# Graph attention on one core: the adjacency rounds taken from behind head 0, two splits moved later, two masks given to VectorE, and filler matmuls in head 0

## The reference

```python
seq = (x @ W_seq).reshape(N, H, DH)
score1 = jnp.einsum('nhd,d->hn', seq, a1)
score2 = jnp.einsum('nhd,d->hn', seq, a2)
scores = leaky_relu(score1[:, :, None] + score2[:, None, :], 0.2)
scores = scores + (1.0 - adj)[None, :, :] * -65500.0
attn = softmax(scores, axis=-1)
hidden = einsum('hij,jhd->ihd', attn, seq).reshape(N, D)
out = layernorm(x + elu(hidden @ W_out + b_out))
```

## Time and profile before

| | |
|---|---|
| median of 3 runs | 538.84 us (537.93 to 538.99) |
| the profiled execution | 538.96 us |
| its span, first to last instruction | 537.0 us |
| mean granted TensorE clock | 0.979 |
| TensorE busy | 513.0 us, 96% |
| VectorE busy | 472.1 us, 88% |
| ScalarE busy | 449.9 us, 84% |
| share of TensorE in the chain that ended last | 72% |

### The profile page before, as it was taken

The page is one execution under the profiler, slowest core; times in us unless marked ns, Lnnn a source line. Parts: engine busy times, 40 slices in busy tenths (PEclk is TensorE's granted clock), DMA queues, the critical chain, the costliest instruction groups (busy, mean ns, idle before and its releaser), DMA issues.

```text
span 537.0 us, 15347 instructions
## 1 busy us (share of the span) xinstructions
PE 513.0 (96%) x6778; PEld 463.7 (86%) x6778; DVE 472.1 (88%) x701; ACT 449.9 (84%) x487; POOL 32.1 (6%) x64
## 2 busy tenths in 40 slices
PE   9999997779999999999999999999999999999993
PEld 7888876669999999999999999999999999744542
DVE  3265999868999989999999999999999899888886
ACT  2677897799998899999999999999997869356664
POOL 3000000000000000000000000000000000024542
PEclk9999999589999999999999999999999999999997
DMA  8999972220202202021020201102022040014443
GB/s 287 374 395 324 362 184 39 84 80 2 80 2 81 81 2 80 2 81 49 35 80 2 81 9 73 81 2 81 2 81 79 4 139 2 1 59 141 134 138 117
DMA packets 30434, 52.76 MB, mean 98 GB/s; under 512 B 18336, under 2 KB 19616, under 8 KB 26400
## 3 DMA queue, kind: packets, MB, share of 16 engines
q1 hardware_dynamic: 29816, 51.26, 28.1%
q10 hardware_dynamic: 552, 0.52, 0.3%
HBM read 43.25 MB, written 4.33 MB: 89 GB/s over the span
## 4 chain that ended last, share of the span: by engine, by line
PE 72%; ACT 17%; DVE 9%; issue 2%; POOLq 0%; POOL 0%; ACTq 0%; DVEq 0%
PE sums L438 31%; PE bank L454 17%; ACT tring L569 12%; PE sums L509 10%; PE sums L361 9%; DVE tring L747 2%; ACT low L624 1%; PE sums L346 1%; ACT Vp L603 1%; DVE Vp L823 1%; PE bank L497 1%; PE sums L338 1%; DVE tring L742 1%; ACT tring L536 1%; DVE xp L817 1%
## 5 line engine op out<-in xcount | busy, mean ns | idle before, releaser
L569 ACT ACTIVATE tring<-abc,ab 128x2048 int8<-128x2048 f32 x149 | 290.3, 2028 | 0.0
L438 PE MATMUL sums<-Vp,tring 128*128 128x132 f16 x4096 | 249.0, 223 | 13.0 <-DVE tring L747 9.3
L438 PEld LDWEIGHTS sums<-Vp,tring 128*128 128x128 fp8e4 x4096 | 241.5, 99 | 17.8 <-DVE tring L747 12.6
L747 DVE TENSOR_TENSOR tring<-adj,tring 128x512 uint32<-128x512 uint32 (+1 forms) x265 | 168.2, 666 | 16.5 <-ACT tring L569 16.3
L454 PE MATMUL bank<-Vp,adj 128*128 128x132 f16 x2048 | 126.7, 222 | 0.7 <-DVE Vp L823 0.7
L454 PEld LDWEIGHTS bank<-Vp,adj 128*128 128x128 fp8e4 x2048 | 122.9, 97 | 1.2 <-DVE Vp L823 1.1
L742 DVE TENSOR_SCALAR tring<-abc,ab 128x2048 int8<-128x2048 f32 x91 | 116.3, 1279 | 0.0
L361 PE MATMUL sums<-Vp,abc 128*128 128x272 f32 x256 | 61.5, 393 | 0.0
L509 PE MATMUL sums<-abc,Vp 128*128 128x512 f32 (+1 forms) x136 | 57.5, 568 | 0.3 <-ACT Vp L670 0.3
L361 PEld LDWEIGHTS sums<-Vp,abc 128*128 128x128 f32 x256 | 47.3, 190 | 8.7
L509 PEld LDWEIGHTS sums<-abc,Vp 128*128 128x128 f32 x136 | 24.7, 190 | 22.9 <-issue 22.0
(11 more groups left out here) (96 smaller groups left out, 315.7 us busy)
## 6 DMA issues: line engine op xcount, KB each, us to landing
Vp<-in_adj_dram SPq DMA_DIRECT2D x16, 1024.0 KB, 7.7
abc<-a_rows SPq DMA_DIRECT2D x15, 1024.0 KB, 4.8
abc<-in_x_dram SPq DMA_DIRECT2D x16, 256.0 KB, 5.6
Vp<-in_x_dram SPq DMA_DIRECT2D x16, 256.0 KB, 3.1
out_dram<-Vp SPq DMA_DIRECT2D x16, 256.0 KB, 2.1
abc<-in_L_gnn_W_out_dram SPq DMA_DIRECT2D x1, 1024.0 KB, 5.4
Vp<-in_L_gnn_W_seq_dram ACTq DMA_DIRECT2D x2, 256.0 KB, 4.8
Vp<-in_L_gnn_W_seq_dram SPq DMA_DIRECT2D x2, 256.0 KB, 5.1
```

What stands on the lines that cost most here:

```text
L438: mm = pe.matmul(bank[b][:, c * 2 * VW:(c + 1) * 2 * VW], slot(jt)[:, it * P:(it + 1) * P].bitcast(F8), Vp[:, h, jt, :, :], start=(jt == 0 ...
L569: return act.activation(slot(jt)[:, columns], row(h)[:, columns], ACT.Sign, bias=ab[:, jt, H + h:H + h + 1], scale=-1.0)
L747: return dve.tensor_tensor(words, adj8[:, jt, columns].bitcast(U32), words, ALU.bitwise_and)
```

## The change

Head 0 has no adjacency rounds any more, heads 1 and 2 have five and head 3 has six; from head 4 on the numbers stay. In head 1 the two rounds among the tiles come after tile 12 and not 7. Head 0 makes the values of head 1 only; those of heads 2 and 3 are made in head 1, those of heads 4 and 5 in head 2. VectorE compares tiles 11 and 13 of head 0 also. In head 1 the sums of head 0 are taken at tile 0 and not 1. For heads 2, 3 and 4 the copies of the rounds behind begin at tile 2 and not 6. TensorE waits for `Mb_ready` before head 0, and runs three filler matmuls into bank 6 after each of the tiles 4 to 14 of head 0. ScalarE's exponential of line 646 moves from tile 5 to tile 9 of head 0.

```diff
-DVE_TILES = ((1, 3, 4, 6, 7, 8), SIX, SEVEN, SEVEN, SIX, SIX, SIX, FIVE, SIX, SIX, SIX, FIVE, SIX, SEVEN, SEVEN, FIVE)
-
-MID, MID_AT = (0,) + (2,) * (H - 1), 7
-ROUNDS = (4, 4, 4, 4, 4, 4, 4, 4, 4, 4, 4, 4, 5, 5, 6, 0)
-
-SPLITS = ((1, 2, 3), (4,), (5,), (6,), (7,), (8,), (9,), (10,), (11,), (12,), (13,), (14,), (15,), (), (), ())
+DVE_TILES = ((1, 3, 4, 6, 7, 8, 11, 13), SIX, SEVEN, SEVEN, SIX, SIX, SIX, FIVE, SIX, SIX, SIX, FIVE, SIX, SEVEN, SEVEN, FIVE)
+
+MID, MID_AT = (0,) + (2,) * (H - 1), (None, 12) + (7,) * (H - 2)
+ROUNDS = (0, 5, 5, 6, 4, 4, 4, 4, 4, 4, 4, 4, 5, 5, 6, 0)
+
+SPLITS = ((1,), (2, 3), (4, 5), (6,), (7,), (8,), (9,), (10,), (11,), (12,), (13,), (14,), (15,), (), (), ())
@@
-SUMS_AT = (None, 1) + (4,) * (H - 2)
-VALUES_AT = ((3, 7, 11),) + ((1,),) * (H - 1)
-HIGH_AT = ((5, 9, 13),) + ((6,),) * (H - 1)
-LOW_AT = ((6, 10, 14),) + ((9,),) * (H - 1)
-
-BEHIND_AT = (None, range(2, NT)) + (range(6, NT),) * (H - 3) + ((5, 6, 8, 9),)
+SUMS_AT = (None, 0) + (4,) * (H - 2)
+VALUES_AT = ((2,), (2, 7), (2, 7)) + ((1,),) * (H - 3)
+HIGH_AT = ((5,), (4, 9), (4, 9)) + ((6,),) * (H - 3)
+LOW_AT = ((6,), (6, 10), (6, 10)) + ((9,),) * (H - 3)
+
+BEHIND_AT = (None,) + (range(2, NT),) * 4 + (range(6, NT),) * (H - 6) + ((5, 6, 8, 9),)
@@ TensorE
-            def warm(n):
+            def warm(n, into=bank[2]):
                 for _ in range(n):
-                    pe.matmul(bank[2][:, 0:2 * P], ones16[:, 0:P], ones16, start=True, stop=True)
+                    pe.matmul(into[:, 0:2 * P], ones16[:, 0:P], ones16, start=True, stop=True)
@@
                 if h == 0:
+                    pe.wait_ge(Mb_ready, 1)
                     for jt in range(EARLY):
@@
                     mask_products(h, jt, range(NT // 2 if h == 0 and jt < EARLY else 0, NT)).then_inc(t_free, 1)
-                    if jt == MID_AT:
+                    if h == 0 and EARLY // 2 <= jt < NT - 1:
+                        warm(3, bank[6])
+                    if jt == MID_AT[h]:
                         for s in round_range(h)[:MID[h]]:
                             adj_products(s)
@@ ScalarE
-                    if h == 0 and jt == 5:
+                    if h == 0 and jt == 9:
                         act.wait_ge(r_in, 1)
```

## The result

The changed kernel takes 549.53 us (median of 4 runs, 548.96 to 549.98) against 538.91 of the kernel before (537.93 to 540.43): a ratio of 1.0198, 95% interval 1.0173 to 1.0222. It is slower, as forecast, but by 10.6 us and not by 6.4. The time lies 0.03 us above the range that I gave. The profiled execution took 549.38 us, with a span of 547.3.

The account below looks back on a forecast made before the run. TensorE bounds the kernel from 116.93 us, masks before. Head 0 ends 7.2 us earlier and 0.7 of slow rounds goes; + 2.55 + 5.8 + 2 x 2.7 + 0.4 gives 545.4 us from 538.96, range 541 to 549.5.

Parts of the forecast that it names:

- step 4: Heads 2 and 3: round copies stand ahead of copy_low in ScalarE's program, so TensorE idles 2.7 us before each head.
- the two gaps: Before heads 2 and 3: TensorE waits for copy_low and the join of the sums, 2.7 us each.
- wait in head 4: Head 4: ScalarE has less lead, so split_low(7) comes late for the round behind tile 7; 0.4 us more.
- Step 1: Head 0: masks all joined at 106.2 us, 8.6 us sooner; products end at 109.7 instead of 116.93, 7.2 us earlier.
- Step 2: Between heads 0 and 1: no rounds hide copy_low and the join of head 0's sums; TensorE waits 2.55 us.
- Step 3: Head 1 up to tile 12: VectorE's 16.8 us of work makes masks bind; TensorE idles 5.8 us in pieces.
- rival (a): The clock falls in the new gaps or returns late in head 0: 547 to 550 us; chance 0.22.
- Rival (b): Faster: late engines find rounds done at the copies, no 2.7 us gaps, TensorE follows head 0's masks: 537.0 us; chance 0.08.

Follow-up runs that it names:

- Experiment 4: The changed kernel with head 0's tiles 11 and 13 compared by ScalarE again, as before the change: 551.25 us, ratio 1.0220 to the kernel before.
- experiment 3: The changed kernel without the three filler matmuls behind tiles 4 to 14 of head 0: 550.39 us, ratio 1.0195 to the kernel before.
- experiment 8: The changed kernel without fillers in head 0 but with 22 fillers in each gap before heads 2 and 3: 546.87 us, ratio 1.0149.
- experiment 1: The changed kernel with the copies of the rounds behind beginning at tile 4 in heads 2 and 3, behind copy_low: 541.62 us, ratio to before 1.0042.
- experiment 5: On top of experiment 1, the sums of head 0 taken at tile 2 of head 1 instead of tile 0: 540.02 us, ratio to before 1.0012.
- Experiment 6: On top of experiment 1, splits of heads 2 and 3 early in head 1, its two rounds behind tile 6 instead of 12: 541.35 us, ratio 1.0029.
- experiment 2: The changed kernel with 22 filler matmuls in each of the gaps before heads 2 and 3: 547.85 us, ratio 1.0148 to the kernel before.
- experiment 7: Changed kernel: copies behind copy_low in heads 2 to 4, head 0's sums at tile 2, head 1 as in experiment 6, fillers only behind tiles 4 to 8: 536.81 us.

## Why the prediction was right and wrong

The way was right, and each step stood where the text put it. What failed is, above all, a term that the sum had at nothing, the half clock behind the gaps of step 4 (1.6 us), and one that it had too small, the handovers from engine to engine (1.1 us over three gaps). With the late start and the rest the sizes add up to 4 us too little:

| step | predicted | measured | difference |
|---|---|---|---|
| start of head 0's products | 84.1 | 84.97 | +0.9 |
| from there to the end of head 0 | 25.6 | 25.3 | -0.3 |
| to the start of head 1 | 2.55 | 2.95 | +0.4 |
| to the end of tile 12 | 17.75 | 18.1 | +0.3 |
| the two gaps | 2 x 2.7 | 2 x 3.05 | +0.7 |
| clock in head 2 | 0 | 1.6 | +1.6 |
| wait in head 4 | 0.4 | 0.77 | +0.4 |

Together 4.0, which is 549.4 - 545.4. All but one point the same way, so they added up.

- **Step 1** was right in its size. Its masks came 22.1 us behind the first product, as worked out. Experiment 4 puts 2.35 of the 8.6 us down to the two comparisons, which TensorE, held by its fillers, could not use. The fillers were costed on the path at 1.65 us beyond tile 10; experiments 3 and 8 show that they cost 0.7 to 0.8 net, since without them TensorE works off the same tiles partly at half clock. The Trainium skill (page "TensorE: Matmul & The Clock Gate", section "What's actually happening") has activity lift the clock. This case's traces agree: behind the fall in head 0 the granted clock was back at 1.00 at 100 to 102 us with the fillers, and in experiment 3 at 104 to 106 us, by the mask products alone.
- **Step 2, and step 4** with it, had the mechanism right; experiment 1 takes both gaps away and gives 7.9 us of the median. The term that was too small is the passing of a wait from engine to engine. I had counted 0.2 us in all, for two handovers. The third, from the join to TensorE, was left out. By the pace, the rows above show 0.19 from a round's end (141.63) to its copy, 0.17 from copy_low's end (144.98) to the join, and 0.19 from the join's end to the first matmul: 0.55. In front of head 1 it is 0.26, 0.17 and 0.18: 0.61. The rows of before would have given more than 0.1, too: 117.03 counts from the end of a row, and by the pace TensorE was done at 116.72, 0.31 earlier; copy_low's pace ends at 118.13, and the join starts at 118.30.
- **Step 3** is borne out by experiment 5: in this order VectorE's queue sets the end, and fewer items behind the sums shorten it one for one. Experiment 6 shows that it need not: with the splits early and the rounds behind tile 6 the last mask is ready 3 us before TensorE comes to it. Of the 6.1 us beyond the pace 1.4 were half clock behind the first gap, which took the place of waiting, as rival (a) said: experiment 4 has no such fall, and its head 1 takes the same 33.36 us up to head 2 (150.59 - 117.23, after 146.57 - 113.21). Tile 11 arrived so late that tile 12 had to follow it, which is the 0.3.
- **Rival (a)** is what the sum left out, and the step that failed: the fall of the clock behind a gap. I gave it 0.22 as a case of its own, with 1.5 us for one fall, near the 1.6 measured, and kept it out of the sum because the gaps stand alone between long dense stretches. That reason does not hold: the three kernels whose gaps were without fillers (after, experiments 3 and 4) each lost time to the clock in head 2, and experiment 3 in head 3 as well, so four of six such gaps were followed by a fall. It is the largest single part of the error, 1.6 of 4.0 us. The Trainium skill (same page, section "HAM oscillation — how this bites in real kernels") would have the clock fall only in longer gaps. This case differs: behind a gap of 3.05 us the block took 9.15 us, and with fillers in the gap 7.54 (experiment 2). Why one gap is followed by a fall and the next is not stays open.
- **The start of head 0** is not part of the change. It scatters by up to 6 us between executions of kernels with the same loading phase, and why was not tried. The range should have had it: in the profiled execution it alone moved the time by 0.9 us, more than the 0.03 us that were missing.
- **Rival (b)** has a price, 537.0 us, that a kernel here comes near: without the gaps, the wait in head 4 and the fillers behind tile 8, and with a better order in head 1, the kernel takes 536.8 us (experiment 7). That is chance: it needed the program changed, its head 0 ends 24.1 us behind the first product where the rival has 23.0, and its head 1 is over 2 us shorter than the rival's. The engines do not reach these copies late by themselves (ScalarE waited 2.48 and 1.61 us at them).

## What to carry to other kernels

When a step moves in an engine's program, ask what it waits for and what stands behind it in that program: a copy that waits for work that is still running, put ahead of the copy on which the next head depends, cost 3 us each time and, once, 1.6 more for the clock. Work out a gap as a chain of engines with a price for each handover, and put the clock behind it into the sum. And when few runs are compared at this level, take the stretch in which the kernels differ, not the whole time.

## What was unexpected of the hardware

A handover between engines by semaphore took 0.17 to 0.26 us in the changed kernel, counted by the pace (0.26 from head 0's last product to copy_low), where I had taken 0.1. One and the same stop of 3.05 us had no effect on the granted clock before head 3 in the changed kernel and in experiment 4, and cost 1.4, 1.5, 1.6 or 2.8 us in the other four cases. The stop of 2.95 us before head 1 stands in all nine profiles of changed kernels: in four of them (experiments 3, 4, 6 and 8) the first three tiles behind it ran at full clock, in experiment 5 0.2 us was lost, and in the others 1.4 or 1.6 us. So the length of a stop alone does not give its price. A stop in the middle of head 1 of 3.1 us by the pace (2.92 in its row, experiment 6) cost 1.4 us, one of 1.8 (1.66 in its row, experiment 7) at nearly the same place nothing.
